# Attention after a routed FFN: a fifth bank for the fourth head's maxima, lent to each unit's closing, and P.V in halves between the pairs of scores

## What is computed

```
def _L0_attn_ref(x, Uq, Vq, bq, Uk, Vk, bk, Uv, Vv, bv):
    B, S, D, H, R = (8, 256, 256, 8, 32)
    DH = D // H
    def _lowrank(xh, U, V, b):
        t = jnp.einsum('bshd,hrd->bshr', xh, V)
        return jnp.einsum('bshr,hdr->bshd', t, U) + b
    b_, s_, _ = x.shape
    xh = x.reshape(b_, s_, H, DH)
    q = _lowrank(xh, Uq, Vq, bq)
    k = _lowrank(xh, Uk, Vk, bk)
    v = _lowrank(xh, Uv, Vv, bv)
    scores = jnp.einsum('bqhd,bkhd->bhqk', q, k) / DH ** 0.5
    attn = jax.nn.softmax(scores, axis=-1)
    out = jnp.einsum('bhqk,bkhd->bqhd', attn, v)
    return out.reshape(b_, s_, D)

x = x + 0.5 * _L0_ffn_ref(_layernorm(x, axis=-1), ...)
x = x + _L0_attn_ref(_layernorm(x, axis=-1), ...)
x = x + 0.5 * _L0_ffn_ref(_layernorm(x, axis=-1), ...)
```

## Time and profile before

| | us |
|---|---|
| median of 3 runs | 4926.08 |
| the runs | 4923.77 to 4930.22 |
| the profiled execution | 4928.43 |
| its span | 4926.1 |
| TensorE busy | 3955.4 (80%) |
| VectorE busy | 3260.9 (66%) |
| ScalarE busy | 2829.5 (57%) |
| POOL busy | 2797.8 (57%) |
| mean granted clock | 0.931 |

### The profile page before, as it was taken

How to read it: one execution, slowest core, us unless ns; L and a number is a source line. 1 busy time by engine, 2 the same in 40 slices (tenths; PEclk the granted TensorE clock), 3 DMA queues, 4 the chain that set the end, 5 groups by cost and what they waited for, 6 DMA issues and landing times. The chain is left out here.

```text
span 4926.1 us, 68711 instructions
## 1 busy us (share of the span) xinstructions
PE 3955.4 (80%) x21202; PEld 1529.9 (31%) x21202; DVE 3260.9 (66%) x3752; ACT 2829.5 (57%) x5585; POOL 2797.8 (57%) x966
## 2 busy tenths in 40 slices
PE   0157486599999999999999999999999999920176
PEld 0134354133333333333333333333333333300133
DVE  8744465677777767767776776776677777549644
ACT  4143364366666666666666666666666666634043
POOL 0011000377777777777777777778777777843111
PEclk9999788699999999999999999999999999965588
DMA  6200599557567665756756575675667666467200
GB/s 222 96 9 5 182 344 327 112 108 162 124 143 157 129 145 116 161 122 137 160 126 142 123 161 123 135 160 124 138 129 157 132 137 126 90 193 247 78 2 8
DMA packets 316561, 676.11 MB, mean 137 GB/s; under 512 B 24780, under 2 KB 208608, under 8 KB 268832
## 3 DMA queue, kind: packets, MB, share of 16 engines
q0 software_dynamic: 48000, 340.81, 34.1%
q1 hardware_dynamic: 234624, 297.04, 21.1%
q10 hardware_dynamic: 33568, 33.69, 2.0%
HBM read 198.90 MB, written 136.48 MB: 68 GB/s over the span
## 5 line engine op out<-in xcount | busy, mean ns | idle before, releaser
L1448 DVE TENSOR_REDUCE at_part_max<-at_ps_max 128x4 f32<-128x2048 f32 x1024 | 2347.9, 2293 | 1020.0 <-PE at_ps_max L1575 1019.1
L1547 ACT ACTIVATE at_probs<-at_ps_s 128x512 f32<-128x512 f32 x4096 | 2234.3, 596 | 1042.8 <-PE at_ps_s L1644 988.3
L1428 POOL TENSOR_TENSOR at_pool_sum<-at_pool_sum,at_probs 128x2048 f32<-128x2048 f32 x448 | 2056.9, 4591 | 302.4 <-DMA at_probs<-at_probs 289.1
L1644 PE MATMUL at_ps_s<-at_qs,at_ks 97*128 97x512 f32 (+1 forms) x4096 | 1715.2, 471 | 71.0 <-ACT at_probs L1547 36.3
L1644 PEld LDWEIGHTS at_ps_s<-at_qs,at_ks 97*128 97x128 f32 (+1 forms) x4096 | 681.9, 188 | 1495.0 <-ACT at_probs L1547 1205.9
L1608 PE MATMUL at_ps_acc<-at_probs,at_v 128*32 128x512 f32 x8192 | 1095.8, 607 | 0.9 <-ACT at_probs L1547 0.9
L1575 PE MATMUL at_ps_max<-at_ks,at_qs 32*128 32x512 f32 x4096 | 524.8, 500 | 90.0 <-DVE at_part_max L1448 43.3
L1405 POOL DMA_DIRECT2D at_probs<-at_probs x320 | 282.4, 882 | 483.9 <-PE at_ps_acc L1608 457.9
L1428 POOL TENSOR_TENSOR at_pool_sum<-at_probs 128x2048 f32<-128x2048 f32 x64 | 292.5, 4570 | 95.6 <-ACT at_probs L1547 95.6
L1575 PEld LDWEIGHTS at_ps_max<-at_ks,at_qs 32*128 32x128 f32 x4096 | 197.9, 183 | 444.0 <-DVE at_part_max L1448 297.1
L238 PE MATMUL s_pt<-s_ident,s_sall 128*128 128x128 f32 x2 | 0.9, 447 | 360.2 <-DVE s_sall L205 360.2
(11 more groups left out here) (193 smaller groups left out, 2466.2 us busy)
## 6 DMA issues: line engine op xcount, KB each, us to landing
at_probs<-at_probs POOLq DMA_DIRECT2D x320, 1024.0 KB, 7.4
qk_parts<-pr_hi SPq DMA_DIRECT2D x32, 1024.0 KB, 6.1
qk_parts<-pr_lo SPq DMA_DIRECT2D x32, 1024.0 KB, 6.1
at_qs<-qk_parts SPq DMA_DIRECT2D x320, 64.0 KB, 2.0
at_ks<-qk_parts SPq DMA_DIRECT2D x80, 256.0 KB
s_x<-in_x SPq DMA_DIRECT2D x16, 1024.0 KB, 7.8
after_ffn<-s_y ACTq DMA_DIRECT2D x16, 1024.0 KB, 8.5
pr_x<-after_ffn SPq DMA_DIRECT2D x8, 2048.0 KB
```

The costliest lines, as they stand in the source:

```text
L1428: nc.gpsimd.tensor_tensor(acc, a, probs[:, c % RING], ALU.add).then_inc(pool_added, 1)
L1448: nc.vector.reduce_max(part_max[:, :, t, c], ps_max[:], AX.X).then_inc(part_max_done, 1)
L1547: nc.scalar.activation(probs[:, c % RING, h], ps_s[:, j % 2], ACT.Exp, scale=SCALE).then_inc(exp_done, 1)
L1644: nc.tensor.matmul(ps_s[:, j % 2], ks[rows, g, h, c * P:(c + 1) * P], qs[rows, un % NQB, h, :], start=True, stop=True).then_inc(scores, 1)
```

## The change

Three things. The bank of `ps_misc` becomes a fifth bank of `ps_max`. The reduction is split in one of heads 0 to 2 (`three_max_done`) and one of head 3 (`part_max_done`), and head 3 alternates between banks 3 and 4 (`last_bank`); step n on TensorE waits for the first of step n - 1 and the second of step n - 2. While the fifth bank is lent to the closing of a unit (steps `CLOSED_N`, 7 to 10), head 3 keeps to bank 3 and step n waits for both parts of step n - 1. The closing is put together so that the bank is free the rest of the time: the sums of the raw chunks move from behind their P.V to `close_z`, which stands at the end of cycle 3; `turn_o` is in cycle 5 instead of 6. And the order of a cycle becomes score, score, `max_four`, P.V of the queries 0 to 255, score, score, turns, P.V of the queries 256 to 511. Chunk 0 has its P.V whole in the second place, since its first matmul starts the accumulation of the bank. `pv_done` comes with the second half; ScalarE copies the accumulator after the fourth exponential of a unit instead of the second.

```diff
--- before.py
+++ after.py
@@ -1195,9 +1195,9 @@
 RAW_CHUNKS = (13, 15)
 DMA_PAIRS = ((3, 4), (5, 6), (7, 8), (9, 10), (11, 12))
 DMA_BEFORE_ADD = (2, 2, 3, 4, 5)
-CLOSE_Z_IN = 3
+CLOSE_IN = 3
 TURN_Z_IN = 4
-TURN_O_IN = 6
+TURN_O_IN = 5
 TURN_MAX_IN = 13
 
 
@@ -1227,6 +1227,12 @@
     ADDS = len(pool_chunks) - 1
     ND = len(DMA_PAIRS)
 
+    CLOSED_N = range(CLOSE_IN + MAX_LEAD, TURN_O_IN + MAX_LEAD + 2)
+
+    def last_bank(n):
+
+        return HG if n % 2 and n not in CLOSED_N else HG - 1
+
     def adds_through(c):
 
         return max(pool_chunks.index(c), 1)
@@ -1259,10 +1265,10 @@
         zT = sb("zT", [P, UQ])
         rz = sb("rz", [P, QT, HG])
         o = sb("o", [P, 2, QT, HG, DH])
-        ps_max = psum("ps_max", [P, HG, 512])
+        ps_max = psum("ps_max", [P, HG + 1, 512])
         ps_s = psum("ps_s", [P, 2, UQ])
         ps_acc = psum("ps_acc", [P, UQ])
-        ps_misc = psum("ps_misc", [P, 512])
+        ps_close = ps_max[:, HG]
 
         consts = sem("consts")
         ones_row = sem("ones_row")
@@ -1272,6 +1278,7 @@
         v_in = [sem(f"v_in{n}") for n in range(NG)]
         load_turn = sem("load_turn")
         max_scores = sem("max_scores")
+        three_max_done = sem("three_max_done")
         part_max_done = sem("part_max_done")
         neg_max_done = sem("neg_max_done")
         max_turned = sem("max_turned")
@@ -1445,8 +1452,11 @@
                     dve.wait_ge(neg_max_done, unit)
                 t, c = divmod(n, QT)
                 dve.wait_ge(max_scores, unit * FOURS + n + 1)
-                nc.vector.reduce_max(part_max[:, :, t, c], ps_max[:], AX.X).then_inc(part_max_done, 1)
+                nc.vector.reduce_max(part_max[:, 0:HG - 1, t, c], ps_max[:, 0:HG - 1], AX.X).then_inc(three_max_done, 1)
+                k = last_bank(n)
+                nc.vector.reduce_max(part_max[:, HG - 1:HG, t, c], ps_max[:, k:k + 1], AX.X).then_inc(part_max_done, 1)
                 if n == FOURS - 1:
+                    dve.wait_ge(three_max_done, unit * FOURS + FOURS)
                     dve.wait_ge(part_max_done, unit * FOURS + FOURS)
                     if not first_unit:
 
...
@@ -1522,6 +1531,8 @@
                         k = (c - RING) % NC
                         if k in pool_chunks:
                             act.wait_ge(pool_added, (unit - before) * ADDS + adds_through(k))
+                        if k in RAW_CHUNKS and before:
+                            act.wait_ge(z_done, unit)
                         if k in dma_sources:
                             d = (un - before) * ND + dma_sources.index(k)
                             act.wait_ge(dma_added[d % 2], (b * (BU * ND // 2) + d // 2 + 1) * 16)
@@ -1537,7 +1548,7 @@
                         act.wait_ge(z_done, n)
                         if un > 1 or not first_batch:
                             act.wait_ge(z_turned, n - 1)
-                        nc.scalar.copy(zT[:], ps_misc[:]).then_inc(zT_done, 1)
+                        nc.scalar.copy(zT[:], ps_close).then_inc(zT_done, 1)
 
                     for j in range(TILES):
                         c, h = divmod(j, HG)
@@ -1546,9 +1557,9 @@
                         act.wait_ge(scores, unit * TILES + j + 1)
                         nc.scalar.activation(probs[:, c % RING, h], ps_s[:, j % 2], ACT.Exp, scale=SCALE
                                              ).then_inc(exp_done, 1)
-                        if carry and j == 1:
+                        if carry and j == PER_CYC - 1:
                             copy_acc(unit)
-                        if carry and j == CLOSE_Z_IN * PER_CYC + 3:
+                        if carry and j == CLOSE_IN * PER_CYC + 3:
                             copy_z(unit)
                         if j == TURN_MAX_IN * PER_CYC and (un + 1 < BU or not last):
                             row_of_max(unit + 1, 1)
@@ -1564,15 +1575,21 @@
 
         @block.tensor
         def _(pe):
-            def scores_for_max(unit, un, n, first_unit=False):
+            def scores_for_max(unit, un, n, first_unit=False, closed=None):
 
                 t, c = divmod(n, QT)
                 if n >= 1 or not first_unit:
 
+                    pe.wait_ge(three_max_done, unit * FOURS + n)
+                if n in CLOSED_N:
                     pe.wait_ge(part_max_done, unit * FOURS + n)
+                elif n >= 2 or not first_unit:
+                    pe.wait_ge(part_max_done, unit * FOURS + n - 1)
+                if n == CLOSED_N[-1] + 1 and closed is not None:
+                    pe.wait_ge(o_done, closed)
                 for h in range(HG):
                     rows = slice(HI_AT[h], HI_AT[h] + DH)
-                    last = nc.tensor.matmul(ps_max[:, h], qs[rows, un % NQB, h, t * P:(t + 1) * P],
+                    last = nc.tensor.matmul(ps_max[:, h if h < HG - 1 else last_bank(n)], qs[rows, un % NQB, h, t * P:(t + 1) * P],
                                             ks[rows, un % BU // NU, h, c * 512:(c + 1) * 512], start=True, stop=True)
                 last.then_inc(max_scores, 1)
 
@@ -1599,43 +1616,47 @@
                     carry = un > 0 or not first_batch
                     g, u = un // NU, un % NU
 
-                    def pv(n, k, c):
-
-                        if c == 0 and carry:
-
-                            pe.wait_ge(oT_done, n)
+                    def pv_half(n, k, c, half):
+
+                        cols = slice(half * UQ // 2, (half + 1) * UQ // 2)
+                        if c == 0:
+                            if half == 0:
+                                return
+                            cols = slice(0, UQ)
+                            if carry:
+
+                                pe.wait_ge(oT_done, n)
                         for h in range(HG):
-                            last = nc.tensor.matmul(ps_acc[h * DH:(h + 1) * DH, :],
-                                                    v[:, k // NU, c, h * DH:(h + 1) * DH], probs[:, c % RING, h],
-                                                    start=(c == 0), stop=(c == NC - 1))
-                        if c in RAW_CHUNKS:
-                            if c == RAW_CHUNKS[0] and carry:
-
-                                pe.wait_ge(o_done, n)
+                            last = nc.tensor.matmul(ps_acc[h * DH:(h + 1) * DH, cols],
+                                                    v[:, k // NU, c, h * DH:(h + 1) * DH], probs[:, c % RING, h, cols],
+                                                    start=(c == 0), stop=(c == NC - 1 and half == 1))
+                        if half == 1:
+                            last.then_inc(pv_done, 1)
+
+                    def close_z(n, k, maxima):
+
+                        pe.wait_ge(part_max_done, maxima)
+                        for c in RAW_CHUNKS:
                             for h in range(HG):
-                                last = nc.tensor.matmul(ps_misc[h * DH:(h + 1) * DH, :], ones[:, 0:DH],
-                                                        probs[:, c % RING, h], start=(c == RAW_CHUNKS[0]), stop=False)
-                        last.then_inc(pv_done, 1)
-
-                    def close_z(n, k):
-
+                                nc.tensor.matmul(ps_close[h * DH:(h + 1) * DH, :], ones[:, 0:DH], probs[:, c % RING, h],
+                                                 start=(c == RAW_CHUNKS[0]), stop=False)
                         pe.wait_ge(pool_added, n * ADDS + ADDS)
                         for h in range(HG):
-                            last = nc.tensor.matmul(ps_misc[h * DH:(h + 1) * DH, :], ones[:, 0:DH],
+                            last = nc.tensor.matmul(ps_close[h * DH:(h + 1) * DH, :], ones[:, 0:DH],
                                                     pool_sum[:, k % 2, h], start=False, stop=True)
                         last.then_inc(z_done, 1)
 
                     def turn_z(n):
                         pe.wait_ge(zT_done, n)
                         for t in range(QT):
-                            last = nc.tensor.transpose(ps_misc[:, t * P:(t + 1) * P], zT[:, t * P:(t + 1) * P], ident[:])
+                            last = nc.tensor.transpose(ps_close[:, t * P:(t + 1) * P], zT[:, t * P:(t + 1) * P], ident[:])
                         last.then_inc(z_turned, 1)
 
                     def turn_o(n):
                         pe.wait_ge(rz_done, n)
                         pe.wait_ge(oT_done, n)
                         for t in range(QT):
-                            last = nc.tensor.transpose(ps_misc[:, t * P:(t + 1) * P], oT[:, t * P:(t + 1) * P], ident[:])
+                            last = nc.tensor.transpose(ps_close[:, t * P:(t + 1) * P], oT[:, t * P:(t + 1) * P], ident[:])
                         last.then_inc(o_turned, 1)
 
                     def score(j):
@@ -1654,7 +1675,7 @@
                             pe.wait_ge(q_in[ahead % NQB], (b * (BU // NQB) + ahead // NQB + 1) * LOADS)
                             if ahead % NU == 0:
```

(49 more changed lines are left out.)

## The result

| | before | after |
|---|---|---|
| median | 4926.21 us | 4951.71 us |
| runs | 4923.77 to 4930.22 (5) | 4947.24 to 4970.53 (5) |
| ratio | | 1.0062, 95% interval 1.0038 to 1.0087 |
| profiled execution, span | 4926.1 | 4948.0 |

The change makes the kernel 0.6% slower. The forecast was 4919 us, a small gain or none; the time lies inside the range of 4840 to 4990, on the other side of no change.

The account below looks back on a forecast made before the run. Score matmuls, P.V and exponentials on two score banks were taken to bound the 3.10 us cycle, not VectorE's maxima. Terms +3 + 4 - 4 - 8 - 2 = -7 us from 4926.08 gave 4919 us, range 4840 to 4990.

Parts of the forecast that it names:

- chain S1, P.V, S2, E2, E3: Attention cycle: second score matmul, P.V, third score matmul, third and fourth exponentials, next second score; 3.11 us, no maximum or VectorE.
- The steady cycle: Ordinary attention cycle after the change: stays 3.10 to 3.11 us, +3 us over 63 units.
- M to the half: TensorE, from the four maximum matmuls to the first half of P.V: 0.43 us, bounds 0.24 and 0.50.
- the half to S2: TensorE, from the first half of P.V to the third score matmul: 0.57 us, bounds 0.50 and 0.67.
- the second half hidden: P.V's second half, after the fourth score matmul, fits before the last exponential frees a bank, with 0.2 us to spare.
- rivals of overlap: Maximum matmuls and P.V overlap, or VectorE was the bound: about 3 us a unit, POOL allows 1.74; 4809 us; chance 0.15.
- dear halves: P.V's halves cost more than half: first half 0.67 us, 0.10 more in 15 cycles of 63 units; 5013 us; chance 0.20.
- Reductions and the lead-in: VectorE's split reduction takes 1.76 and 0.69 us; the stretch ahead of the first unit gets 8 us shorter.
- The unit: Closing of a unit in one piece, turns moved: 3.37 us over 16 cycles for 3.31, +0.06 a unit, +4 us over 63.
- the closing needs POOL's last addition about 3 us later: TensorE's closing asks for POOL's sum later, so waits of 26.3 us over 13 matmuls shrink by about 4 us.
- Outside the steady part: Ahead of the first unit, steps fall from 3.20 to 2.67 us, -8 us; last unit, without maxima, -2 us.
- third rival: Closing in one piece costs more: 2.6 us without exponentials, then a copy; 0.5 us more a unit, 4950 us; chance 0.10.

Follow-up runs that it names:

- light reduction: Kernel before with VectorE's maximum reduction reading 256 of the 512 columns of each bank: 4900.59 us, ratio 0.9954.
- third score bank: Kernel before with the closing in one piece and its bank lent to the scores for 12 of 16 cycles, maxima in four banks: 4812.51 us, ratio 0.9768.
- pair of kernels without loops: Changed kernel and kernel before, each with the attention's batch loop written out on all five engines: 4905.40 us (ratio 0.9963) and 4901.80 us (0.9950).

## Why the prediction was wrong

**What bounds the kernel: right.** The chain S1, P.V, S2, E2, E3 was read from a cycle, a stretch after the turns and the last unit. The light reduction and the third score bank both bear it out, from opposite sides.

**The steady cycle: right.** M to the half 0.43, the half to S2 0.57, the second half hidden, 3.11. The rivals of overlap and of dear halves are both refuted by the same rows. The Trainium skill, "TensorEngine Tiling (Array Packing)", section "Tiling Modes", which the prediction weighed, states that a change of tiling mode drains TensorE. That M to P.V costs the full 0.43 agrees with it.

**Reductions and the lead-in: right.** 1.76 and 0.68 for 1.76 and 0.69. The first score comes 9.5 us earlier for 8 forecast; the kernels here that keep the lead-in of before have it at 927.0 to 931.9 us, so that 1.5 us mean little. A step ahead of unit 0 is 0.80 + 1.86 = 2.66 us, where the earlier trace rows has 3.20:

```profile
905.25 0.80 PE L1592 MATMUL at_ps_max<-at_ks,at_qs 32*128 32x512 f32 x4 [1.86 <-DVE at_part_max L1455]
```

The text ahead has the granted clock at 1.00 over nearly all of the attention. In this stretch it is 0.50 in both kernels (868 to 930 us before, 868 to 920 after), and four matmuls of a maximum take 0.80 us there and 0.50 in the units.

**The unit: mechanism right, size off.** 53.12 against 53.0; +0.20 over before and not +0.06, which is 9 us over all units. Of the cycles, 3 took 5.6 where I had 5.5.

**POOL: the step "the closing needs POOL's last addition about 3 us later" failed.** I moved the closing later against the start of cycle 3, and the first DMA of a unit by 1.24 only. But the piece in cycle 3 pushes the DMA in cycle 5 back as well. Counted from the second score of a unit, in the median of the units, TensorE asks for the sum 2.1 us later than before, while the first DMA starts 2.45 later and the last addition ends 3.1 later: the slack fell from 3.1 to 2.1 us. The waits rose from 26.3 to 39.3 us, in the matmuls' row alone from 10.1 to 14.6, where I had them shrink by 4; 3 of these 4.5 us are in the last unit:

```profile
  POOL at_pool_sum L1435: 39.3, 21
```

**The step "Outside the steady part" left out the batch boundaries, and that decided.** The prediction prices the stretch ahead of unit 0 and the last unit, and takes 63 units as alike. They are not: at each of the five jumps back the trace of before has TensorE idle for 3.6 us and its clock down behind it, 26 us in all, and this change altered that price. Measured, +20 us in the profiled executions, and 22 us by the pair of kernels without loops. Term by term from the table of the result: +20 at the boundaries, where the prediction had nothing; +13 for the units, where it had +7; -9.5 ahead of them for -8; +1 in the other units, where POOL's waits were to give -4; and -2 for the last unit and the end together, as forecast. That is -7 + 20 + 6 - 2 + 5 = +22 us, where 22 (spans) and 25 (medians) were measured. My third rival, the closing in one piece, comes nearest with 4950, by luck: it had its price at every unit, 0.5 us. With the bank and the closing alone a unit grew by 0.3 and the kernel by nothing that the measurement can tell; a larger price, 3.2 us, was paid once, where the piece fell into the longest cold stretch. Nor is it the sum's merit that the time lies inside the range of 4840 to 4990, for no term of it covered the boundaries.

**Open.** Why the standstill at a jump is 4.8 us after and 3.6 before is not settled: each part alone moves it (2.6 to 3.1 with the bank, 3.6 to 4.9 with the halves; the branch takes 3.4 to 3.8 and 4.3 to 5.6), and no run separates the number of TensorE's instructions from what stands last. Nor is it known why the cold stretch lasted four cycles at one of the five jumps, or why it is longer after the change at all. The changed kernel's runs lie in two groups, three at 4947 to 4952 and two at 4970. The slower two have the lower mean granted clock (0.924 and 0.925 against 0.926 to 0.929), so more time at the lower level; the trace is of a run of the faster group, and no trace shows where the 20 us went. One more long stretch like the one above, some 6 us over the others, would not be enough.

## What to carry to other kernels

A releaser in the profile is the semaphore that came last, not the bound: measure the slack of a wait by the shortest time in which the same wait is ever served (here 2.35 us against 2.55), and look for a stretch in which one of the parties is missing. When a resource comes free, spend it on the chain that was found, and not on the wait that is named: the same bank changed nothing that can be told on the maxima (ratio 1.0006) and gave -2.3% on the scores. And price the seams of a loop, not only its body: list the longest iterations before calling them alike.

## What the runs showed of the hardware that I had not expected

TensorE's sequencer spends 3.4 to 6.4 us in the branch that jumps back to the start of a loop body of some 430 us, and 0.08 in the one that does not jump. ScalarE and VectorE stand still at their own jumps too, for 2.8 to 6.3 and 3.0 to 5.7 us in the changed kernel with TensorE's loop written out. No trace shows such a standstill of POOL at its jump. With the loop written out on all five engines, the one kernel gave back 25 us and the other 46; written out on TensorE alone, 5 and 7, since in the changed kernel the other engines' jumps took over. A standstill of 2.6 to 5.5 us on TensorE was followed at every jump back of the kernel before, the changed one and its two parts by a granted clock of 0.50, for 3.4 to 13.7 us and once for 23.9, though TensorE was busy all through most of it (5.00 of 5.00 us in each stretch from 3515 to 3530).
